# Small jobs inside the attention stage, each issued in two pieces behind two output quads instead of whole behind one, in a new order

## The chip, the core and the metric

The kernel runs on one core of a Trainium2 chip, in one launch. The metric is the device time in microseconds: the median of three runs of the kernel before is 269.8 us (269.74 to 269.80). Engines are named as in the profile: PE is TensorE's matrix multiplication, PEld its weight loads, ACT ScalarE, DVE VectorE, POOL GpSimd, SP SyncE, which issues the transfers.

## The reference

For 2 x 1024 tokens of width 128 the reference computes a gated feed-forward layer, causal attention, and the feed-forward layer again, each on a layer norm of x and each added to x:

```
x = x + 0.5 * ffn(layernorm(x));  x = x + attention(layernorm(x));  x = x + 0.5 * ffn(layernorm(x))

ffn:       gate from rms-normed logits of 8 experts (softmax, top 1, normalised to nearly 1)
           out = sum over e of (gelu(x @ w1[e] + b1[e]) @ w2[e] + b2[e]) * gate,   128 -> 256 -> 128
attention: q, k, v = split((xn * ln_w + ln_b) @ w_qkv), 8 heads of 8 columns; q and k to unit length
           softmax(8 * q @ k.T, causal) @ v, then @ w_out
```

All arrays are float32.

## The kernel before

**Groups and stages.** The 2048 tokens are four groups of 512 (four tiles of 128). The first layer runs group by group over 16 chunks of hidden units (three matmuls up, three down, with every operand in a high and a low part). Its last chunks run into the attention stage, and the second layer follows with the same 16-chunk loop. The second layer's groups are numbered 4 to 7 (`GROUPS` is 4).

**The attention stage** is a list of 80 steps, two to a *quad step*, so 40 quad steps. A unit is one group's queries with four of the heads. There are eight units: 3, 3, 7, 7, 3, 3, 7, 7 quad steps long, and two units make a pair (pairs start at quads 0, 6, 20 and 26, called `q1`, `q2`, `q3` from the second on). A step is: scores on PE (L708) into one of three sets of PSUM banks, the exponential on ACT (L937), for blocks on the causal diagonal a mask on POOL (L1527, L1533), and for both steps of a quad together the product with the values on PE (L746, for a unit's last quad, the corners, L740). The scores of a step wait until the exponential three steps earlier is done. A unit's last quad has small exponentials (128x256 instead of 128x1024). PE's program is fixed: in quad step k it issues the scores of steps 2k and 2k + 1 and then the output of quad k - 3, called here the output behind those scores. At the end of a unit the output stands between the two scores instead.

**The jobs** (`jobs`, `fill`, `empty`) are small pieces of other work that PE does behind the output of a given quad, into one spare PSUM bank: the transposes of the fourth group's normalised tokens (`"ln"`), its q, k, v products in two halves (`"qkv"`), the output projections of an earlier pair in two halves (`"project"`), and the transposes for the second layer's first group (`"ffn_ln"`). DVE empties the bank after each (`empty`), and runs `output(pair)` before the first job of a pair: it transposes the pair's outputs out of PSUM (`o_copied`), divides, and transposes back (`o_ready`), which is what the projections read. The bank is one, so `fill(n)` begins with `pe.wait_ge(job_emptied, n)`: all earlier jobs must have been emptied. DVE's order is the loop over `jobs` at the end of its program, with the work that each `if` adds behind a job: behind the second `qkv` half stand squares, sums, the guess and nine Newton operations, and the unit vectors (`own_squares` to `unit_vectors`), then `stacks`, which the transposing DMAs for pair 3's scores read. Behind other jobs stand statistics and normalising of the second layer's groups (`first_stats`, `normalise`, L1028, L1037, L1044) and `turn_features`, a DVE transpose that SP sends through DRAM to transposed features. POOL takes the reciprocal root of the variance (`ln_once`) in its own fixed place among the masks.

Of the kernel before, what the change touches and what calls it, by code (L numbers as in the profile page):

```python
# [30 lines left out]
P = 128  # L31
# [3 lines left out]
GROUP_TILES = 4  # L35
# [13 lines left out]
QUADS = 2  # L49
# [34 lines left out]
AT_FIRST = dict(AT, gate_product=6, gate_logits=6, gate_shift=11, gate_tanh=13, gate_weight=14, ln_copy=4, ln_low=8,  # L84
# [27 lines left out]
def build(nc, x, ln_w, ln_b, w_qkv, w_out, gate_w, gate_b, rms_w, w1, b1, w2, b2, out):  # L112
# [9 lines left out]
    with ctx:  # L122
# [128 lines left out]
        for st in steps:  # L251
# [13 lines left out]
        jobs = [(q1, "ln", LAST), (q1 + 2, "project", (0, 0)), (q1 + 4, "project", (0, 1)),  # L265
                (q1 + 5, "qkv", 0), (q1 + 7, "qkv", 1), (q2 + 3, "ffn_ln", 0),
                (q2 + 5, "project", (1, 0)), (q3, "project", (1, 1)),
                (q3 + 2, "project", (2, 0)), (q3 + 4, "project", (2, 1)),
                (quad_steps, "project", (pairs - 1, None))]
        assert len({at for at, *_ in jobs}) == len(jobs)  # L270
# [25 lines left out]
        def job_bank(n):  # L296

            at = jobs[n][0]
            return 13 - output_bank(steps[2 * min(at, quad_steps - 1)]["unit"] // QUADS)

        def pair_of_job(n):
            return steps[2 * min(jobs[n][0], quad_steps - 1)]["unit"] // QUADS
# [241 lines left out]
        def _(pe):  # L544
# [82 lines left out]
            def ffn_group(layer, g):  # L627
# [5 lines left out]
                for c in range(CHUNKS):  # L633
# [12 lines left out]
                    if layer == 1 and first and c == 3:  # L646
                        fill(len(jobs) - 1)
# [65 lines left out]
            def pv(k):  # L713
# [10 lines left out]
                if opens and pair > 1:  # L724
                    pe.wait_ge(job_emptied, sum(at < k for at, *_ in jobs))
# [26 lines left out]
            def fill(n):  # L752

                at, kind, arg = jobs[n]
                bank = ps[:, job_bank(n), :]
                if n:
                    pe.wait_ge(job_emptied, n)
                gates = sum(quad < at for quad in gate_at)
                if gates:
                    pe.wait_ge(gate_logits_done, GROUPS + gates)  # L760
                if n == 0 or pair_of_job(n) != pair_of_job(n - 1):
                    pe.wait_ge(o_copied, pair_of_job(n))
                tiles = [slice(P * i, P * i + P) for i in range(GROUP_TILES)]
                if kind in ("ln", "ffn_ln"):
                    norm = ATT if kind == "ln" else FFN
                    pe.wait_ge(xn_done[norm], GROUP_TILES * (LAST + 1 if kind == "ln" else GROUPS + 1))
                    for i, tile in enumerate(tiles):
                        m = pe.transpose(bank[:, tile], xn[:, norm, i, :], ident[:, :])
                elif kind == "qkv":
                    for i in halves[arg]:  # L770
                        m = pe.matmul(bank[:, 192 * (i % 2):192 * (i % 2) + 192], xf[:, ATT, tiles[i]], wqkv_sb[:, :],
                                      start=True, stop=True)
                elif kind == "project":
                    pair, half = arg
                    pe.wait_ge(o_ready, pair + 1)
                    for tile in tiles if half is None else [tiles[i] for i in halves[half]]:
                        m = pe.matmul(bank[:, tile], o_feat[:, tile], wout_sb[:, :], start=True, stop=True)  # L777
                m.then_inc(job_filled, 1)


# [24 lines left out]
            next_job = 0  # L805

# [12 lines left out]
            def outputs(k):  # L819

                nonlocal next_job
                for quad in range(max(pv_until(k - 1), 0), pv_until(k)):
# [5 lines left out]
                    if jobs[next_job][0] == quad:  # L828
                        fill(next_job)
                        next_job += 1  # L830
                    if quad in gate_at:
                        pe.wait_ge(job_emptied, next_job)
# [189 lines left out]
        def _(dve):  # L1022
# [162 lines left out]
            def ffn_group(layer, g):  # L1185
# [7 lines left out]
                for c in range(CHUNKS):  # L1193
# [194 lines left out]
            for n, (at, kind, arg) in enumerate(jobs[:-1]):  # L1388
# [6 lines left out]
                if (kind, arg) == ("project", (0, 1)):  # L1395
# [168 lines left out]
```

## Time and profile before

| | |
|---|---|
| median of 3 runs | 269.8 us |
| the profiled execution, its own time | 269.82 us |
| its span, first to last instruction | 268.1 us |
| first layer, to the first exponential | 104.7 us |
| attention stage, to ACT's table load for the second layer | 67.9 us (104.7 to 172.5) |
| second layer | 95.6 us |
| granted TensorE clock | 0.998 of full speed (2.4 GHz) |
| PE, DVE, ACT, POOL busy | 258.2, 216.2, 217.5, 80.7 us |

What is timed is the execution, 269.82 us. The span is what the instructions cover, and 1.7 us lie around it. In a timeline row the first number is the start, the second how long the merged instructions were busy, xN how many records there are, and brackets give the idle time before and what ended it. A float32 matmul is two records (two passes), so "x4" for a projection half is two matmuls. Records on PE overlap, so the distance between the starts of two rows says more of a cost than the busy time does.

### The profile page before, as it was taken

To read this page: it belongs to the slowest core of one execution; us is meant where nothing else is said; L and a number is where in the kernel's file an instruction comes from. 1 tells how busy PE (TensorE), PEld (TensorE's weight loads), DVE (VectorE), ACT (ScalarE), POOL (GpSimd) and SP (SyncE) were. 2 spreads that over 40 slices of the span, in tenths; PEclk is the share of its full clock that TensorE was granted. 3 is DMA by queue.
4 is the path that set the end of the run, shared out by engine and by line. 5 is a ranking of instruction groups with operands and counts; after the bars stand their busy time and mean duration, and the time that the engine had idled before them with its cause. 6 is when DMAs were issued, how large, how long until landed. Compare 5 with 4: busy or idle time off the path is not lost.

```text
span 268.1 us, 5428 instructions
## 1 busy us (share of the span) xinstructions
PE 258.2 (96%) x1829; PEld 183.6 (69%) x1829; DVE 216.2 (81%) x590; ACT 217.5 (81%) x344; POOL 80.7 (30%) x175
## 2 busy tenths in 40 slices
PE   7999999999999999979998999999999999999995
PEld 6886878888788786533434433378888887888783
DVE  7999899998898987797378587378889678697784
ACT  2897668859878889999999999987777867859673
POOL 6302104204850482664349545520200000200100
PEclk9999999999999999999999999999999999999999
DMA  5741200001012104101314003300004211210311
GB/s 152 219 123 23 58 1 2 0 1 39 2 34 46 42 2 78 40 1 22 62 39 82 2 4 78 80 1 4 0 8 111 42 39 39 39 34 9 80 39 39
DMA packets 33343, 11.51 MB, mean 43 GB/s; under 512 B 24130, under 2 KB 32548, under 8 KB 33316
## 3 DMA queue, kind: packets, MB, share of 16 engines
q1 hardware_dynamic: 33172, 11.11, 17.7%
q8 instruction: 14, 0.23, 0.4%
q14 instruction: 13, 0.11, 0.1%
q10 hardware_dynamic: 144, 0.07, 0.1%
HBM read 4.88 MB, written 2.62 MB: 28 GB/s over the span
## 4 chain that ended last, share of the span: by engine, by line
PE 73%; DVE 8%; ACT 7%; issue 5%; POOL 4%; DMA 2%; SPq 0%; POOLq 0%; DVEq 0%; ACTq 0%
PE ps L590 10%; PE ps L596 10%; PE ps L608 10%; PE ps L593 10%; PE ps L613 10%; PE ps L611 9%; PE ps L746 5%; ACT probs L937 3%; PE ps L708 2%; PE ps L777 2%; ACT h L924 2%; POOL probs L1533 1%; POOL w_raw L1527 1%; DMA kT<-k_stack 1%; DVE h_lo L1100 1%
## 5 line engine op out<-in xcount | busy, mean ns | idle before, releaser
L924 ACT ACTIVATE h<-ps,cols 128x512 f32<-128x512 f32 x128 | 88.0, 694 | 36.2 <-PE ps L596 32.6
L1100 DVE TENSOR_TENSOR h_lo<-h,h_hi 128x512 fp32r<-128x512 f32 x128 | 88.6, 698 | 19.1 <-ACT h_hi L927 16.7
L937 ACT ACTIVATE probs<-ps 128x1024 f32<-128x1024 f32 (+1 forms) x80 | 65.0, 918 | 1.5 <-PE ps L708 1.4
L590 PE MATMUL ps<-xT_hi,w_hi 128*128 128x512 f32 x128 | 51.5, 402 | 0.0
L608 PE MATMUL ps<-h_hi,w_hi 128*128 128x512 f32 x128 | 50.5, 395 | 0.3 <-ACT yT L949 0.3
L927 ACT ACTIVATE h_hi<-ps,cols 128x512 fp32r<-128x512 f32 x73 | 50.2, 688 | 0.0
L613 PE MATMUL ps<-h_lo,w_hi 128*128 128x512 f32 x128 | 50.2, 392 | 0.0
L596 PE MATMUL ps<-xT_lo,w_hi 128*128 128x512 f32 x128 | 49.9, 390 | 0.0
L593 PE MATMUL ps<-xT_hi,w_lo 128*128 128x512 f32 x128 | 49.9, 390 | 0.0
L611 PE MATMUL ps<-h_hi,w_lo 128*128 128x512 f32 x128 | 49.9, 389 | 0.0
L746 PE MATMUL ps<-probs,v_ones 128*32 128x512 f32 (+4 forms) x384 | 34.2, 458 | 0.9 <-POOL probs L1533 0.6
L1436 POOL TENSOR_TENSOR gate_rms<-gate_ms,neg_half 128x4 f32<-128x4 f32 x8 | 9.7, 1217 | 72.8 <-DVE gate_ms L1065 72.7
L608 PEld LDWEIGHTS ps<-h_hi,w_hi 128*128 128x128 f32 x128 | 24.0, 188 | 6.3 <-ACT yT L949 0.7
L613 PEld LDWEIGHTS ps<-h_lo,w_hi 128*128 128x128 f32 x128 | 24.0, 188 | 6.0 <-DVE h_lo L1100 0.9
L590 PEld LDWEIGHTS ps<-xT_hi,w_hi 128*128 128x128 f32 x128 | 24.0, 188 | 5.7 <-issue 0.7
L596 PEld LDWEIGHTS ps<-xT_lo,w_hi 128*128 128x128 f32 x128 | 24.0, 188 | 5.2
L611 PEld LDWEIGHTS ps<-h_hi,w_lo 128*128 128x128 f32 x128 | 24.0, 188 | 4.8
L593 PEld LDWEIGHTS ps<-xT_hi,w_lo 128*128 128x128 f32 x128 | 24.1, 188 | 4.5
L1098 DVE CAST h_hi<-h 128x512 fp32r<-128x512 f32 x55 | 23.4, 426 | 3.9 <-ACT h L924 3.1
L1533 POOL TENSOR_SCALAR_AFFINE_SELECT probs<-probs 128x128 f32<-128x128 f32 x64 | 18.0, 312 | 21.2 <-ACT probs L937 20.8
L708 PE MATMUL ps<-qT,kT 32*64 32x64 f16 (+5 forms) x320 | 19.9, 266 | 2.3 <-ACT probs L937 1.1
L708 PEld LDWEIGHTS ps<-qT,kT 32*128 32x128 f16 (+1 forms) x320 | 7.2, 96 | 20.1 <-ACT probs L937 12.4
(141 smaller groups left out, 273.2 us busy)
## 6 DMA issues: line engine op xcount, KB each, us to landing
w_raw<-in_L_ffn_w SPq DMA_DIRECT2D x8, 256.0 KB, 4.6
turned<-blocks SPq DMA_DIRECT2D x6, 256.0 KB, 2.0
w_raw<-turned SPq DMA_DIRECT2D x24, 64.0 KB, 2.3
w_raw<-v_ones SPq DMA_DIRECT2D x8, 128.0 KB, 2.4
x_sb<-in_L_attn_x SPq DMA_DIRECT2D x3, 256.0 KB, 6.8
out_x<-x_sb SPq DMA_DIRECT2D x3, 256.0 KB, 2.3
w_raw<-o_scaled SPq DMA_DIRECT2D x2, 256.0 KB, 4.3
x_sb<-in_L_attn_x SPq DMA_DIRECT2D x2, 128.0 KB, 2.3
```

What stands on the lines that cost most here:

```text
L590: pe.matmul(bank, w1_hi[:, w], xT_hi[:, cols_g], start=True, stop=False)
L593: pe.matmul(bank, w1_lo[:, w], xT_hi[:, cols_g], start=False, stop=False)
L596: pe.matmul(bank, w1_hi[:, w], xT_lo[:, cols_g], start=False, stop=True).then_inc(up_done, 1)
L608: pe.matmul(y, w2_hi[:, w], h_hi[:, c % RING, :], start=(c == 0), stop=False)
L611: pe.matmul(y, w2_lo[:, w], h_hi[:, c % RING, :], start=False, stop=False)
L613: pe.matmul(y, w2_hi[:, w], h_lo[:, c % RING, :], start=False, stop=(c == CHUNKS - 1)).then_inc(down_done, 1)
L708: m = pe.matmul(ps[first_row:first_row + keys, 2 * score_set(s) + hd, at:at + width], kT[rows, kp, st["quad"], k0:k0 + keys], qT[rows, p, ...
L746: m = pe.matmul(ps[ROW * j:ROW * j + ROW, bank, q0:q0 + width], v_ones[:, SEQ // P * st["b"] + kt, 4 * st["quad"] + j, :], probs[:, (s + j ...
L924: first = nc.scalar.activation(h[:, slot, :], ps[:, BANK_H + slot, :], ACT.Gelu, bias=bias)
L927: nc.scalar.activation(h_hi[:, slot, :], ps[:, BANK_H + slot, :], ACT.Gelu, bias=bias).then_inc(gelu_done, 1)
L937: nc.scalar.activation(probs[:, s % P_SLOTS, :, 0:width], ps[:, bank:bank + 2, 0:width], ACT.Exp, scale=SCALE).then_inc(exp_done, 1)
L1100: dve.tensor_tensor(h_lo[:, slot, :], h[:, slot, :], h_hi[:, slot, :].bitcast(f32), ALU.subtract).then_inc(split_done, 1)
```

## The change

Each job has two quads instead of one. `fill(n, piece)` issues the first half of the job behind the output of its first quad and the second half behind its second quad. The wait for the bank stands ahead of the first piece, and the count that releases DVE (`job_filled`) behind the second. The order of jobs changes:

| job | quad before | quads after |
|---|---|---|
| ln (fourth group) | 6 | 6, 7 |
| qkv first half | 11 | 8, 10 |
| qkv second half | 13 | 11, 12 |
| project (0,0) | 8 | 13, 14 |
| project (0,1) | 10 | 15, 17 |
| project (1,0) | 25 | 21, 23 |
| project (1,1) | 26 | 24, 25 |
| ffn_ln | 23 | 27, 28 |
| project (2,0) | 28 | 31, 32 |
| project (2,1) | 30 | 34, 35 |

The last job, project (3), stays behind chunk 3 of the second layer. The first gate product moves from quad 24 to 30, its tanh on ACT from step 62 to 72. DVE: `stacks` of the fourth group moves behind the emptying of project (0,0), the normalising of group 4 behind (1,1), and the normalising and turning of group 6 leave the attention stage for chunk 1 of the second layer. In that layer's first group ACT's copy of features moves from chunk 4 to 9, DVE's low part from 8 to 10. POOL: the roots for groups 4 and 5 stand together behind the masks of quad 25, that of group 6 behind all masks.

```diff
+AT_FIRST = dict(AT, gate_product=6, gate_logits=6, gate_shift=11, gate_tanh=13, gate_weight=14, ln_copy=9, ln_low=10,
                 ln_stats=(5, 6), ln_aggregate=7, ln_normalise=(12, 13))
...
+        jobs = [((q1, q1 + 1), "ln", LAST), ((q1 + 2, q1 + 4), "qkv", 0), ((q1 + 5, q1 + 6), "qkv", 1),
+                ((q1 + 7, q1 + 8), "project", (0, 0)), ((q1 + 9, q1 + 11), "project", (0, 1)),
...
+        pieces_at = {quad: (n, piece) for n, (quads, *_) in enumerate(jobs[:-1]) for piece, quad in enumerate(quads)}
-        gate_at = {q2 + 4: GROUPS, quad_steps - 3: GROUPS + 1}
+        gate_at = {q3 + 4: GROUPS, quad_steps - 3: GROUPS + 1}
-        TANH_AT = 62
+        TANH_AT = 72
...
-            def fill(n):
+            def fill(n, piece):
+                quads, kind, arg = jobs[n]
                 bank = ps[:, job_bank(n), :]
-                if n:
-                    pe.wait_ge(job_emptied, n)
...
+                if piece == 0:
+                    if n:
+                        pe.wait_ge(job_emptied, n)
+                    gates = sum(quad < quads[0] for quad in gate_at)
+                    if gates:
+                        pe.wait_ge(gate_logits_done, GROUPS + gates)
+                    if n == 0 or pair_of_job(n) != pair_of_job(n - 1):
+                        pe.wait_ge(o_copied, pair_of_job(n))
...
                 elif kind == "qkv":
-                    for i in halves[arg]:
-                        m = pe.matmul(bank[:, 192 * (i % 2):192 * (i % 2) + 192], xf[:, ATT, tiles[i]], wqkv_sb[:, :],
-                                      start=True, stop=True)
+                    i = halves[arg][piece]
+                    m = pe.matmul(bank[:, 192 * piece:192 * piece + 192], xf[:, ATT, P * i:P * i + P], wqkv_sb[:, :],
+                                  start=True, stop=True)
...
-                m.then_inc(job_filled, 1)
+                if piece:
+                    m.then_inc(job_filled, 1)
...
                     pv(quad)
-                    if jobs[next_job][0] == quad:
-                        fill(next_job)
-                        next_job += 1
+                    if quad in pieces_at:
+                        fill(*pieces_at[quad])
...
+                        if c == 1:
+                            normalise(FFN, GROUPS + 2, 2)
+                            turn_features(GROUPS + 2)
...
                 if (kind, arg) == ("qkv", 1):
                     own_squares(LAST)
...
                     unit_vectors(dve, LAST)
+                if (kind, arg) == ("project", (0, 0)):
                     stacks(LAST)
```

PE's program behind the outputs of quads 14 and 15, before (`ps<-qT,kT` is scores, `ps<-probs,v_ones` an output):

```order
L746 MATMUL ps<-probs,v_ones 32x512 x4
L708 MATMUL ps<-qT,kT 128x320 x2
L708 MATMUL ps<-qT,kT 128x192 x2
L708 MATMUL ps<-qT,kT 128x320 x2
L708 MATMUL ps<-qT,kT 128x192 x2
L746 MATMUL ps<-probs,v_ones 32x512 x4
L708 MATMUL ps<-qT,kT 64x64 x8
L746 MATMUL ps<-probs,v_ones 32x512 x4
```

and after, where L778 is a piece of a projection:

```order
L747 MATMUL ps<-probs,v_ones 32x512 x4
L778 MATMUL ps<-wout_sb,o_feat 128x128
L709 MATMUL ps<-qT,kT 128x320 x2
L709 MATMUL ps<-qT,kT 128x192 x2
L709 MATMUL ps<-qT,kT 128x320 x2
L709 MATMUL ps<-qT,kT 128x192 x2
L747 MATMUL ps<-probs,v_ones 32x512 x4
L778 MATMUL ps<-wout_sb,o_feat 128x128
L709 MATMUL ps<-qT,kT 64x64 x8
L747 MATMUL ps<-probs,v_ones 32x512 x4
```

The first L778 is the second piece of project (0,0), behind quad 14. The second is the first piece of project (0,1), behind quad 15 and ahead of a corner's scores; being a first piece, it carries a wait for the bank. Nothing stood in either place before.

DVE's program at the end of the fourth group's chain, before:

```order
L413 SCALAR_TENSOR_TENSOR rnorm<-newton,rnorm 128x64
L440 TENSOR_TENSOR qkn<-qk_raw,rnorm 128x512
L1182 CAST q_stack<-qkn 128x32x16
L1182 CAST k_stack<-qkn 128x64x8
L456 TENSOR_TENSOR q_stack<-qkn,q_stack 128x32x8
L456 TENSOR_TENSOR k_stack<-qkn,k_stack 128x32x8
L1044 TENSOR_SCALAR xn<-x_sb,mean_var,rstd 128x128 x4
```

and after (L1353 is the emptying of a projection):

```order
L413 SCALAR_TENSOR_TENSOR rnorm<-newton,rnorm 128x64
L440 TENSOR_TENSOR qkn<-qk_raw,rnorm 128x512
L1353 TENSOR_TENSOR x_sb<-ps,x_sb 128x256
L1178 CAST q_stack<-qkn 128x32x16
L1178 CAST k_stack<-qkn 128x64x8
L456 TENSOR_TENSOR q_stack<-qkn,q_stack 128x32x8
L456 TENSOR_TENSOR k_stack<-qkn,k_stack 128x32x8
L1353 TENSOR_TENSOR x_sb<-ps,x_sb 128x256
```

The emptying of project (0,0) has come between the chain and the stacks; before, both halves of that projection were emptied ahead of the fourth group's copies.

## Rows read from the trace of the kernel before

**Rows 1.** Windows of four stretches, busy us and instructions of each engine

```profile
104.70:172.60 67.90, 63.56 (x887) 26.70 (x886) 45.99 (x152) 66.33 (x86) 36.02 (x101) 1.00 0.18 38
...
180.00:200.00 20.00, 20.00 (x94) 16.67 (x93) 16.74 (x42) 14.92 (x25) 1.73 (x2) 1.00 0.00 1
```

**Rows 2.** Waits between 120 and 173 us: total, times, longest

```profile
PEld ps L708 <- ACT probs L937: 11.3, 17, 0.8
```

**Rows 3.** Timeline of ACT in narrow windows: start, us, instruction, [idle before]

```profile
119.59 4.73 ACT L937 ACTIVATE probs<-ps 128x1024 f32<-128x1024 f32 x5
...
126.90 4.22 ACT L937 ACTIVATE probs<-ps 128x256 f32<-128x256 f32 x5 [0.47 <-PE ps L708]
...
137.76 1.59 ACT L937 ACTIVATE probs<-ps 128x1024 f32<-128x1024 f32 x3
...
139.38 1.03 ACT L937 ACTIVATE probs<-ps 128x1024 f32<-128x1024 f32 x1
...
162.68 9.82 ACT L937 ACTIVATE probs<-ps 128x1024 f32<-128x1024 f32 x12
```

**Rows 4.** Timeline of PE, first half of the attention stage

```profile
121.27 0.66 PE L768 MATMUL ps<-ident,xn 128*128 128x128 f32 x4
...
124.78 0.71 PE L777 MATMUL ps<-wout_sb,o_feat 128*128 128x128 f32 x4
125.42 0.25 PE L708 MATMUL ps<-qT,kT 32*64 32x64 f16 x8
...
126.60 0.58 PE L708 MATMUL ps<-qT,kT 32*64 32x64 f16 x12
...
128.75 0.40 PE L708 MATMUL ps<-qT,kT 32*128 32x512 f16 x4
129.08 1.07 PE L746 MATMUL ps<-probs,v_ones 128*32 128x320 f32 x16
130.08 0.92 PE L771 MATMUL ps<-wqkv_sb,xf 128*128 128x192 f32 x4
130.93 0.40 PE L708 MATMUL ps<-qT,kT 32*128 32x512 f16 x4
131.25 0.64 PE L740 MATMUL ps<-w_raw 128*32 128x128 f32 x16
```

**Rows 5.** Timeline of PE, the last projection job

```profile
182.07 1.05 PE L777 MATMUL ps<-wout_sb,o_feat 128*128 128x128 f32 x8
182.87 0.47 PE L590 MATMUL ps<-xT_hi,w_hi 128*128 128x512 f32 x1
```

**Rows 6.** Timeline of PE where the after-job scores of 138.6 us stand

```profile
138.61 0.92 PE L708 MATMUL ps<-qT,kT 32*64 32x64 f16 x16
```

**Rows 7.** Timeline of DVE: a projection's add, then the fourth group's chain

```profile
125.52 0.42 DVE L1354 TENSOR_TENSOR x_sb<-ps,x_sb 128x256 f32<-128x256 f32 x1
...
134.70 0.42 DVE L1339 COPY qk_raw<-ps 128x256 f32<-128x256 f32 x1 [2.98 <-PE ps L771]
...
141.08 0.52 DVE L1182 CAST q_stack<-qkn 128x512 f16<-128x512 f32 x1
```

**Rows 8.** Timeline of DVE: statistics, normalising, the output's first transpose

```profile
142.96 1.10 DVE L1044 TENSOR_SCALAR xn<-x_sb,mean_var,rstd 128x128 f32<-128x128 f32 x4
143.99 0.70 DVE L1310 STREAM_TRANSPOSE o_blocks<-ps 128x512 f32<-128x512 f32 x1
...
156.67 0.87 DVE L1028 BATCH_NORM_STATS2 bn_part<-x_sb 128x6 f32<-128x128 f32 x4
157.58 0.38 DVE L1037 BATCH_NORM_AGGREGATE mean_var<-bn_part 128x2 f32<-128x6 f32 x4
```

**Rows 9.** Timeline of PE, later jobs

```profile
153.80 1.06 PE L746 MATMUL ps<-probs,v_ones 128*32 128x512 f32 x8 [0.19 <-DVE x_sb L1354]
```

**Rows 10.** Timeline of DVE in the first group of the second layer

```profile
179.32 0.71 DVE L1310 STREAM_TRANSPOSE o_blocks<-ps 128x512 f32<-128x512 f32 x1
```

**Rows 11.** Timeline of PE there

```profile
185.48 0.39 PE L613 MATMUL ps<-h_lo,w_hi 128*128 128x512 f32 x1
```

More of the change, by code:

```diff
@@ L264, in build @@
         q1, q2, q3 = first_of_pair[1:]
[L265 to L270, printed above, removed]
+        jobs = [((q1, q1 + 1), "ln", LAST), ((q1 + 2, q1 + 4), "qkv", 0), ((q1 + 5, q1 + 6), "qkv", 1),
+                ((q1 + 7, q1 + 8), "project", (0, 0)), ((q1 + 9, q1 + 11), "project", (0, 1)),
+                ((q2 + 1, q2 + 3), "project", (1, 0)), ((q2 + 4, q2 + 5), "project", (1, 1)),
+                ((q3 + 1, q3 + 2), "ffn_ln", 0), ((q3 + 5, q3 + 6), "project", (2, 0)),
+                ((q3 + 8, q3 + 9), "project", (2, 1)), ((quad_steps, quad_steps), "project", (pairs - 1, None))]
         job_number = {(kind, arg): n for n, (_, kind, arg) in enumerate(jobs)}
-        gate_at = {q2 + 4: GROUPS, quad_steps - 3: GROUPS + 1}
+        pieces_at = {quad: (n, piece) for n, (quads, *_) in enumerate(jobs[:-1]) for piece, quad in enumerate(quads)}
+        gate_at = {q3 + 4: GROUPS, quad_steps - 3: GROUPS + 1}
         LATER_GATES = {0: GROUPS + 1, 2: GROUPS + 2, 3: GROUPS + 3}
-        TANH_AT = 62
+        TANH_AT = 72
         def gate_of(layer, g):
@@ L296, in job_bank @@
         def job_bank(n):
-            at = jobs[n][0]
+            at = jobs[n][0][0]
             return 13 - output_bank(steps[2 * min(at, quad_steps - 1)]["unit"] // QUADS)
         def pair_of_job(n):
-            return steps[2 * min(jobs[n][0], quad_steps - 1)]["unit"] // QUADS
+            return steps[2 * min(jobs[n][0][0], quad_steps - 1)]["unit"] // QUADS
         by_dma = [("features", F) for F in range(GROUPS + 1, 2 * GROUPS)] + [("y", F) for F in range(GROUPS, 2 * GROUPS - 1)]
@@ L724, in pv @@
                 if opens and pair > 1:
-                    pe.wait_ge(job_emptied, sum(at < k for at, *_ in jobs))
+                    pe.wait_ge(job_emptied, sum(quads[1] < k for quads, *_ in jobs))
                     pe.wait_ge(gate_logits_done, GROUPS + sum(quad < k for quad in gate_at))
@@ L775, in fill @@
                     pe.wait_ge(o_ready, pair + 1)
-                    for tile in tiles if half is None else [tiles[i] for i in halves[half]]:
-                        m = pe.matmul(bank[:, tile], o_feat[:, tile], wout_sb[:, :], start=True, stop=True)
-                m.then_inc(job_filled, 1)
+                    for i in halves[piece] if half is None else halves[half][piece:piece + 1]:
+                        m = pe.matmul(bank[:, P * i:P * i + P], o_feat[:, P * i:P * i + P], wout_sb[:, :], start=True, stop=True)
+                if piece:
+                    m.then_inc(job_filled, 1)
             def keep_busy(times):
@@ L827, in outputs @@
                     pv(quad)
-                    if jobs[next_job][0] == quad:
-                        fill(next_job)
-                        next_job += 1
+                    if quad in pieces_at:
+                        fill(*pieces_at[quad])
                     if quad in gate_at:
-                        pe.wait_ge(job_emptied, next_job)
+                        pe.wait_ge(job_emptied, sum(quads[1] <= quad for quads, *_ in jobs))
                         gate_product(gate_at[quad], 13 - output_bank(steps[2 * quad]["unit"] // QUADS))
@@ L1387, in _ @@
             normalise(ATT, LAST, LAST)
-            for n, (at, kind, arg) in enumerate(jobs[:-1]):
+            for n, (_, kind, arg) in enumerate(jobs[:-1]):
                 if n == 0 or pair_of_job(n) != pair_of_job(n - 1):
```

46 lines of the change are left out of this document (17 added, 29 removed).

## The prediction

> **What bounds the kernel now.** First the table of windows by stage. In the second layer PE has no idle time and ACT and DVE do, so PE sets the pace. In the attention stage, where nearly all of the edit lies, ACT is busy 66.3 of 67.9 us and PE 63.6 [rows 1]. The waits say which is the slower: PE's weight loads for the scores wait for exponentials 17 times, 11.3 us in total [rows 2]. So ACT paces the stage and PE runs ahead of it, by the three sets of banks at most. Then ACT's timeline in narrow windows, for the pace itself: five big exponentials in 4.73 us with the last of them about 1.1 long is 0.90 each. In the row of three at 137.76, two small ones follow a big one at 0.90 and the next exponential starts at 139.38, 1.62 later, so a small one takes about 0.26 and about 0.19 is lost at this unit's end [rows 3]. What the change can give back is only what ACT loses beyond that pace. From 139.38 to 162.68 lie 28 exponentials (steps 40 to 67), 22 big and 6 small: 22 x 0.904 + 6 x 0.264 + 0.13 for a tanh = 21.6 us, where 23.3 passed, so 1.7 us are lost [rows 3]. The clearest loss is earlier: the small exponential at 126.90 had waited 0.47 [rows 3], for scores that stand behind an output, which stands behind a projection of 0.64 us [rows 4].
>
> **What a piece costs.** Whole jobs, by the distance of starts: projection 124.78 to 125.42, 0.64; qkv half 130.08 to 130.93, 0.85; the four transposes 0.59 (busy 0.66, less the 0.07 by which the projection's busy time also passes its distance) [rows 4]. How much of that is not work shows in the last projection job: eight records took 0.80 where four took 0.64, but it is followed by matmuls of its own shape (128 wide), not by scores of 32 rows [rows 5]. So a record is worth about 0.10 and 0.24 of the four-record job is fixed. The Trainium skill has the reason, in "TensorEngine Tiling (Array Packing)", under Key Properties of Tiling Modes: changing the tiling mode drains TensorE. The rows fit that. If only records cost, a piece would be half a job, 0.32, the chain below would be 0.4 us shorter, and the sum 0.4 lower.
>
> I take 0.43 for half a projection, 0.52 for one product of a qkv half, 0.37 for two transposes. No row shows one alone; the ends are half a job (0.32, no fixed part) and 0.13 more than I take (0.56, near the whole). Ten jobs in pieces add 6 x 0.22 + 2 x 0.19 + 2 x 0.15 = 2.0 us to PE. Most of it is covered while PE waits for ACT (11.3 us of such waits), and single pieces fit: a full quad costs PE 0.33 for scores and 1.00 for the output (128.75, 129.08, 130.08) [rows 4], with a piece 1.76, under ACT's 1.81. That is the good side: a whole projection makes 1.97.
>
> **The first part, to the fourth group's products.** From the first transposes at 121.27 on PE: 0.37, then 1.33 + 0.37, 1.33 + 0.52, so the corner's scores at 125.19 (before 125.42), 0.23 early. From the second set of corner scores at 126.60 to the next scores at 128.75 it was 2.15 with a projection of 0.64; with a product of 0.52 it ends at 128.40. Then 1.33 + 0.52 = 130.25 (before 130.93), 0.33 for scores, 0.58 for the corner output (131.25 on), 0.52: the second products are done at T = 131.68. Before it was 134.6, so the chain behind it starts 2.9 us earlier [rows 4, 7].
>
> **The step that decides.** Behind project (0,0) comes project (0,1), at quad 15, and its first piece waits until project (0,0) is emptied. DVE empties that only after the fourth group's chain. In the trace the chain from the first copy to the end of the unit vectors lasts 134.70 to 141.08, 6.38 us, and a projection's add 0.42 [rows 7]. So the bank is free at 131.68 + 0.10 + 6.38 + 0.42 + 0.02 = 138.60. PE comes to the wait after two quads with a piece and one without: 131.68 + 1.76 + 1.76 + 1.33 = 136.53. It stands 2.07 us. Queued behind it are the scores of the unit's corner and everything after. Those come at 138.60 + 0.43; 0.18 for them (125.42's row less overlap), 1.00 for the output, and the second corner scores and those of the next unit start at 140.21. Before, they started at 138.61 [rows 6], so 1.6 late. At a corner reached late like this, ACT's next big exponential starts 0.61 behind (126.60 to 126.90, and a small one of 0.31): 140.82 instead of 139.38 [rows 3, 4, 6]. This is +1.44 us. Bounds: if T comes 0.5 us sooner (pieces at half price) +0.9; if each of the six pieces before T costs 0.13 more, +2.2. More waiting by ACT elsewhere before this point is free, since the chain on DVE hides it.
>
> **Behind it.** Of the 1.7 us lost between 139.38 and 162.68 about 0.6 is the end of three units, which stays. The rest hangs on whole jobs late in the stage: transposes, the gate product, two projections behind one another with the wait of 0.19 for an emptying [rows 9], two more. Pieces fit under ACT's pace, so I give back 0.7 and not the full 1.1, because a new wait comes in. The transposes at quad 27 need `o_copied`, and DVE reaches that transpose only after the emptying of (1,1), a normalising of 1.1 and statistics of 0.87 + 0.3, then its own 0.70 [rows 8]. With (1,1) done at 152.64 on the old clock, that is 152.7 + 0.44 + 1.15 + 1.20 + 0.72 = 156.2, and PE arrives at 152.64 + 0.5 (the wait of quad 26's output) + 1.00 + 1.33 = 155.5. It stands 0.7; ACT, with big exponentials queued, sees little of it, but a unit's end follows. Then the tanh falls outside this stretch, +0.13, and the piece at quad 32 now stands between a corner's output and a full one, which I price at +0.2. Together -0.7 + 0.3 = -0.4.
>
> The moved stacks end at about 138.6 + 2.0 = 140.6 (they take 141.08 to 142.96), where they ended by 142.96 before, and the scores that need them come later than before, not earlier, so their transfers are no wait: 0 [rows 7, 8]. Second layer: normalising (1.1) and turning (0.7, as L1310) come upon DVE behind output(3), which starts at 179.32 and occupies it about 2.2 us [rows 8, 10]. Then chunk 5's low part is due at 185.48, when PE starts the matmul that reads it [rows 11]: DVE reaches it at 179.32 + 2.2 + 0.6 + 1.8 = 183.9 and ends at 184.6. That hides it, with 0.9 us left. If the cover is gone it costs up to 1.
>
> **Sum.** The profiled execution took 269.82 us, its span 268.1. Change: +1.44 - 0.4 = +1.04. Predicted 270.9 us; the median of the runs shown, 269.8, is the same to 0.02.
>
> **Rivals.** *Faster: the wait never bites.* If the bank is free before PE arrives, the pieces do what their size suggests. From the first part ACT is 0.5 early at 139.38 and 0.4 comes later: 268.9. It decides at DVE's chain: it would have to last 2.1 us less than the 6.8 shown. Against it, the chain is fifteen operations that depend on one another, behind three copies, and PE is late by at most 0.5. Chance 0.12. *No change.* The wait costs nearer to 0.9, with the full 1.1 given back afterwards: 269.8 + 0.9 - 1.1 + 0.3 = 269.9. For it, bounds on both sides are real. Chance 0.17. *Slower still.* The wait at quad 27 is seen in full (+0.7), and DVE's backlog in the second layer reaches PE (+0.5): 272.1. For it, DVE order is fixed and both stand behind long groups of work. Chance 0.14. That leaves 0.57 for the forecast.
>
> **The numbers.** Less than 0.2%, 0.54 us, can't be told from no change here. The forecast's own range is 270.1 to 271.7; from bounds, 0.9 - 1.1 + 0.3 is +0.1 and 2.2 - 0.4 + 0.7 is +2.5. The range for 8 in 10 is 269.5 to 272.2, leaving out the faster case and the end of the slow one. Slower by over 0.2%: the forecast's 0.57, of which 0.03 falls short, and the slow rival 0.14, and so 0.68; the same 0.20, faster 0.12.
>
> **What would show it.** In the new profile, PE's wait before a piece of L778 with DVE's L1353 as its end, some 2 us, near 136.5 to 138.6; the next big exponential near 140.8; a single projection piece to the next scores 0.43; the second products done near 131.7; PE waiting for o_blocks before the transposes of ffn_ln, 0.7; PE without idle time in the second layer, and its length unchanged at 95.6 us within 0.2. It is wrong if that first wait is under 1 us, or if ACT reaches step 40 before 140, or if the second layer grows.

## The result, and the profile after

The changed kernel took 271.61 us (median of 6 runs, 271.51 to 271.70), the kernel before 269.78 on the same chip (6 runs, 269.74 to 269.87). The ratio is 1.0067, with an interval of 1.0054 to 1.008. It is slower by 1.83 us, where +1.1 was forecast against that median; the time lies inside the stated range, 269.5 to 272.2. Times here are medians of fast executions; of the kernel with the gate's transpose moved (below) one execution of 629.66 us, in the slow state, is left out. The profiled execution took 271.70 us with a span of 269.9; 1.8 us of span came in, so the span holds the whole difference.

The line numbers move a little: PE's scores, outputs, projections, qkv products and transposes are L709, L747, L778, L772 and L769 now, ACT's exponential is L933, DVE's add of a projection L1353, POOL's diagonal mask L1531. The windows of the same two stretches (span of the stretch, then busy us and instructions of PE, its weight loads, DVE, ACT and POOL, granted clock, DMA share, GB/s):

```profile
104.70:173.64 68.94, 64.29 (x887) 26.76 (x886) 42.79 (x147) 66.02 (x85) 35.98 (x98) 1.00 0.16 33
180.00:200.00 20.00, 20.00 (x94) 16.68 (x93) 18.36 (x46) 14.24 (x24) 1.61 (x2) 1.00 0.12 27
```

Beside [rows 1]: ACT's load of its next table, which ends the attention stage, starts at 173.64 where it started at 172.52, ACT is busy for about as long as before, and PE still has no idle time in the second layer (20.00 of 20.00 us). From the first matmul of the second layer to the end it was 94.45 us and is 94.44. So all that is lost is lost before that matmul (it stood at 173.61, and stands at 175.50: +1.89).

The waits between 120 and 175 us (total, times, longest) answer [rows 2]:

```profile
PEld ps L709 <- ACT probs L933: 6.7, 13, 0.8
...
ACT probs L933 <- PE ps L709: 2.6, 5, 0.8
...
PEld ps L747 <- POOL probs L1531: 2.0, 5, 1.1
...
PE ps L778 <- DVE x_sb L1353: 1.4, 1, 1.4
```

PE's waits for exponentials fell from 11.3 us to 6.7, as they would if pieces fill what was slack. The last line is the wait that the prediction put at quad 15. PE's timeline there (start, us, instruction, and in brackets the idle time before it with its end):

```profile
131.32 0.59 PE L772 MATMUL ps<-wqkv_sb,xf 128*128 128x192 f32 x2
131.84 0.47 PE L709 MATMUL ps<-qT,kT 32*128 32x512 f16 x4
...
133.66 0.49 PE L709 MATMUL ps<-qT,kT 32*128 32x448 f16 x8
...
135.50 0.48 PE L709 MATMUL ps<-qT,kT 32*128 32x320 f16 x8
135.91 1.07 PE L747 MATMUL ps<-probs,v_ones 128*32 128x512 f32 x8
138.40 0.49 PE L778 MATMUL ps<-wout_sb,o_feat 128*128 128x128 f32 x2 [1.42 <-DVE x_sb L1353]
138.81 0.26 PE L709 MATMUL ps<-qT,kT 32*64 32x64 f16 x8
...
139.99 0.59 PE L709 MATMUL ps<-qT,kT 32*64 32x64 f16 x16
```

and DVE's, whose chain of the fourth group ends ahead of the add that frees the bank:

```profile
131.95 0.42 DVE L1338 COPY qk_raw<-ps 128x256 f32<-128x256 f32 x1 [2.59 <-PE ps L772]
...
137.31 0.69 DVE L440 TENSOR_TENSOR qkn<-qk_raw,rnorm 128x512 f32<-128x512 f32 x1
137.92 0.42 DVE L1353 TENSOR_TENSOR x_sb<-ps,x_sb 128x256 f32<-128x256 f32 x1
```

The add ends at 138.34 and the piece starts at 138.40. ACT's timeline, in narrow windows, shows what becomes of it: the small exponentials at 139.12 and 140.30 wait 0.8 each, and the big one of step 40, which stood at 139.38 [rows 3], starts at 140.61, +1.23. Step 68, at 162.68 before, starts at 163.11.

```profile
139.12 0.38 ACT L933 ACTIVATE probs<-ps 128x256 f32<-128x256 f32 x1 [0.83 <-PE ps L709]
...
140.61 1.02 ACT L933 ACTIVATE probs<-ps 128x1024 f32<-128x1024 f32 x1
...
163.11 1.03 ACT L933 ACTIVATE probs<-ps 128x1024 f32<-128x1024 f32 x1
...
165.04 1.02 ACT L933 ACTIVATE probs<-ps 128x1024 f32<-128x1024 f32 x1
...
167.36 1.02 ACT L933 ACTIVATE probs<-ps 128x1024 f32<-128x1024 f32 x1 [0.37 <-PE ps L709]
```

Of these, 163.11 to 165.04 is 1.93 us for two big exponentials and 165.04 to 167.36 is 2.32, where the same two gaps had been 1.82 and 1.81. PE's timeline shows the first reason, at quad 31:

```profile
162.73 1.07 PE L747 MATMUL ps<-probs,v_ones 128*32 128x320 f32 x16
164.22 0.46 PE L778 MATMUL ps<-wout_sb,o_feat 128*128 128x128 f32 x2 [0.42 <-issue]
164.61 0.40 PE L709 MATMUL ps<-qT,kT 32*128 32x512 f16 x4
```

"Issue" names no releaser, but the piece waits by the program for the gate product's bank to be read, and DVE reads it at just that time, behind a normalising and a turning:

```profile
161.66 1.51 DVE L1040 TENSOR_SCALAR xn<-x_sb,mean_var,rstd 128x128 f32<-128x128 f32 x4
163.21 0.71 DVE L1103 STREAM_TRANSPOSE blocks<-xn 128x512 f32<-128x512 f32 x1
163.85 0.27 DVE L1052 STREAM_TRANSPOSE gate_rows<-ps 128x128 f32<-128x128 f32 x1
```

The normalising itself is slow here: four tiles take 1.51 us from 161.66, beside four masks of POOL between 161.26 and 163.57, where the four from 154.31 take 1.11. Those 0.40 us are nearly the whole of the piece's wait of 0.42. No run moves them, so that they cause it is not shown.

The last loss stands at the very end of the stage, on POOL. The exponentials are done before 173.64, and the last big output waits for two diagonal masks. First the kernel before, PE's and POOL's timelines:

```profile
172.61 1.07 PE L746 MATMUL ps<-probs,v_ones 128*32 128x320 f32 x16
```

```profile
172.01 0.54 POOL L1533 TENSOR_SCALAR_AFFINE_SELECT probs<-probs 128x128 f32<-128x128 f32 x2 [0.38 <-ACT probs L937]
```

and the changed one, PE, POOL (each mask in a window of its own) and DVE:

```profile
174.50 1.07 PE L747 MATMUL ps<-probs,v_ones 128*32 128x320 f32 x16 [0.82 <-POOL probs L1531]
```

```profile
173.14 0.58 POOL L1531 TENSOR_SCALAR_AFFINE_SELECT probs<-probs 128x128 f32<-128x128 f32 x1 [0.38 <-ACT probs L933]
...
173.67 0.77 POOL L1531 TENSOR_SCALAR_AFFINE_SELECT probs<-probs 128x128 f32<-128x128 f32 x1
```

```profile
173.17 0.39 DVE L1117 CAST xT_hi<-w_raw 128x512 fp32r<-128x512 f32 x1
173.60 0.69 DVE L423 TENSOR_TENSOR xT_lo<-w_raw,xT_hi 128x512 fp32r<-128x512 f32 x1
```

Two masks took 0.54 together and take 1.31. What changed is DVE's company: the high and low features of group 5 (L1117, L423) had run at 167.86 and 168.32, in slack, and now run beside the masks. They don't wait for what they read, which was turned at 163.21. They come late by their place in DVE's order, behind the emptying of project (2,1), which moved from quad 30 to 34 and 35 and ends at 170.94, and behind `gate_weight` and the statistics.

The whole loss in one ledger, start to start: +1.23 up to step 40; -0.80 from step 40 to 68 (22.50 us where 23.30 passed, 0.13 of it the tanh that left this stretch); +0.11 and +0.51 over steps 68 to 72; +0.07 from there to the load of ACT's table (the same tanh now stands in it); +0.77 from the table load to the last big output. The sum is +1.89, which is what the first matmul of the second layer shows.

### The profile page after: what moved, and what is told of

It reads as the page before. It is cut to its first block, busy times and chain, and to the rows that moved or that the text cites. A ratio compares the mean times of both kernels' runs of the same rounds, so it can differ in the third digit from the quotient of the medians.

```text
span 269.9 us, 5427 instructions
## 1 busy us (share of the span) xinstructions
PE 259.6 (96%) x1829; PEld 184.5 (68%) x1829; DVE 214.9 (80%) x590; ACT 217.1 (80%) x344; POOL 83.0 (31%) x175
## 4 chain that ended last, share of the span: by engine, by line
PE 76%; ACT 7%; DVE 6%; issue 5%; POOL 3%; DMA 1%; POOLq 0%; DVEq 0%; ACTq 0%
PE ps L590 10%; PE ps L596 10%; PE ps L608 10%; PE ps L593 10%; PE ps L613 9%; PE ps L611 9%; PE ps L747 7%; ACT probs L933 4%; PE ps L709 3%; POOL probs L1531 2%; ACT h L920 1%; POOL w_raw L1525 1%; PE ps L778 1%; PE ps L741 1%; DVE h_lo L1096 1%
## 5 line engine op out<-in xcount | busy, mean ns | idle before, releaser
L933 ACT ACTIVATE probs<-ps 128x1024 f32<-128x1024 f32 (+1 forms) x80 | 64.9, 922 | 2.9 <-PE ps L709 2.8
L747 PE MATMUL ps<-probs,v_ones 128*32 128x512 f32 (+4 forms) x384 | 34.2, 458 | 1.5 <-POOL probs L1531 1.5
L1531 POOL TENSOR_SCALAR_AFFINE_SELECT probs<-probs 128x128 f32<-128x128 f32 x64 | 19.7, 337 | 25.8 <-ACT probs L933 25.5
L709 PE MATMUL ps<-qT,kT 32*64 32x64 f16 (+5 forms) x320 | 18.9, 267 | 1.4 <-ACT probs L933 0.6
L747 PEld LDWEIGHTS ps<-probs,v_ones 128*32 128x32 f32 x384 | 9.2, 109 | 13.9 <-issue 6.9
```

The costliest lines, as they stand in the source:

```text
L709: m = pe.matmul(ps[first_row:first_row + keys, 2 * score_set(s) + hd, at:at + width], kT[rows, kp, st["quad"], k0:k0 + keys], qT[rows, p, ...
L747: m = pe.matmul(ps[ROW * j:ROW * j + ROW, bank, q0:q0 + width], v_ones[:, SEQ // P * st["b"] + kt, 4 * st["quad"] + j, :], probs[:, (s + j ...
L933: nc.scalar.activation(probs[:, s % P_SLOTS, :, 0:width], ps[:, bank:bank + 2, 0:width], ACT.Exp, scale=SCALE).then_inc(exp_done, 1)
```

## The experiments

Each time is a median of 4 to 11 executions. The kernel before had a median of 269.77 to 269.82 us beside them, so times are compared with 271.61 and 269.8 throughout. Each interval reaches some 0.3 us to either side, so that a smaller difference between two experiments tells little without the trace.

**The bank freed early.** The theory: quad 15's piece waits for DVE's chain, and that costs most of the loss. The add that empties (0,0) is put behind the first of three Newton rounds; nothing else moves.

```diff
 guesses(LAST)
-inverse_lengths(dve, LAST)
-unit_vectors(dve, LAST)
+inverse_lengths(dve, LAST, range(1))
 ...
 if (kind, arg) == ("project", (0, 0)):
+    inverse_lengths(dve, LAST, range(1, 3))
+    unit_vectors(dve, LAST)
     stacks(LAST)
```

> The changed kernel, with DVE emptying project (0,0) after the first of the three Newton rounds of the fourth group instead of after its unit vectors. In the changed kernel PE stood from 136.9 to 138.4 us before the first piece of project (0,1), and step 40's exponential came 1.23 us later than before. Theory W (the wait for the bank is the largest cost): PE has no wait there, step 40 starts near 138.9 (1.7 earlier than in the changed kernel), the later part gives back less since there is less to give, and the time falls by 1.0 to 1.7 us, to 270.0 to 270.6. Rival P (the price is the 2 us of added work of the pieces on PE, and the wait only stands where PE would lose it anyway): the wait goes and the time falls by under 0.3 us, to 271.3 or more.

Measured: 270.08 us (ratio to before 1.0011, 1.0002 to 1.002), 1.53 less than the changed kernel. PE's timeline, the same piece:

```profile
136.76 0.49 PE L778 MATMUL ps<-wout_sb,o_feat 128*128 128x128 f32 x2
137.18 0.25 PE L709 MATMUL ps<-qT,kT 32*64 32x64 f16 x8
```

and ACT's:

```profile
138.98 1.02 ACT L933 ACTIVATE probs<-ps 128x1024 f32<-128x1024 f32 x1
```

No wait is left, and step 40 starts 0.40 before the old 139.38. So the wait cost 1.53, more than the 1.23 that step 40 is late, because it also hid a small gain of the first part. It doesn't make the kernel faster than before by itself, as the rival of a wait that never bites had it: other costs remain.

**The features early again.** The theory: the masks stretch because DVE works beside them. `early_features` moves ahead of `gate_weight`.

```diff
 if (kind, arg) == ("project", (2, 1)):
+    early_features(GROUPS + 1)
     gate_weight(GROUPS)
 ...
-early_features(GROUPS + 1)
 gate_logits(GROUPS + 1)
```

> The changed kernel, with DVE's cast and subtraction for the features of group 5 put right behind the last projection of the attention stage, ahead of the gate weight and the statistics of group 6. In the changed kernel these two ran at 173.2 to 174.3 us, beside POOL's last diagonal masks, which took 0.58 and 0.77 us instead of 0.29, and PE's second last output came at 174.50, 0.77 later than ACT's end alone would give. Theory M (DVE's operations from SBUF to SBUF in their fast form hold up POOL's masks, and these are on the path): the last two masks take 0.29 each, the second last output comes near 173.7, and the time falls by 0.6 to 0.8 us, to 270.8 to 271.0. Rival L (POOL's masks are late for another reason, or the up matmuls wait for ACT's last exponentials and table load, whatever the masks do): masks get shorter or not, and the time stays within 0.2 us of 271.6.

Measured: 270.77 us (1.0039, 1.0027 to 1.0052), 0.84 less. POOL's timeline and DVE's:

```profile
171.10 1.48 POOL L1531 TENSOR_SCALAR_AFFINE_SELECT probs<-probs 128x128 f32<-128x128 f32 x4 [0.37 <-ACT probs L933]
172.93 0.54 POOL L1531 TENSOR_SCALAR_AFFINE_SELECT probs<-probs 128x128 f32<-128x128 f32 x2 [0.35 <-ACT probs L933]
```

```profile
170.66 0.42 DVE L1117 CAST xT_hi<-w_raw 128x512 fp32r<-128x512 f32 x1
171.11 0.83 DVE L423 TENSOR_TENSOR xT_lo<-w_raw,xT_hi 128x512 fp32r<-128x512 f32 x1
```

The last two masks take 0.54 again. The stretch hasn't gone: it follows the two operations to the masks at 171.10, where PE has other work.

**The same cost put into the kernel before.** If the company of these two operations is the cause, the old kernel must pay for it too. There they are held back until the masks of step 76 are done.

```diff
+dve.wait_ge(mask_done, masks_until[76])
 early_features(GROUPS + 1)
```

> The kernel before, with one edit: DVE's cast and subtraction for the features of group 5 wait until the mask of step 76 is done, so that they stand beside the last two diagonal masks, as in the changed kernel. Nothing else moves. Theory M: the last two masks (0.29 each before, 172.0 to 172.6 us) stretch to 1.0 to 1.4 us together, PE's second last output comes 0.5 to 0.8 us later and the time rises by 0.5 to 0.8, to 270.3 to 270.6. Rival L: the time stays at 269.8, since the masks had time to spare or the two engines don't hold each other up.

Measured: 270.31 us (1.0017, 1.0008 to 1.0026), +0.49. POOL, DVE, and PE:

```profile
172.22 0.99 POOL L1534 TENSOR_SCALAR_AFFINE_SELECT probs<-probs 128x128 f32<-128x128 f32 x2 [0.38 <-ACT probs L937]
```

```profile
171.87 0.43 DVE L1121 CAST xT_hi<-w_raw 128x512 fp32r<-128x512 f32 x1 [4.07 <-POOL probs L1534]
172.33 0.72 DVE L423 TENSOR_TENSOR xT_lo<-w_raw,xT_hi 128x512 fp32r<-128x512 f32 x1
```

```profile
173.26 1.07 PE L746 MATMUL ps<-probs,v_ones 128*32 128x320 f32 x16 [0.50 <-POOL probs L1534]
```

One of the two masks is stretched (0.99 for both, 0.54 before), PE waits 0.50, and the kernel is 0.49 slower. With the experiment before it, this shows the cause from both sides.

**The gate's transpose ahead of the turning.** The theory: the piece at quad 31 waits for DVE's read of the gate product.

```diff
 normalise(FFN, GROUPS + 1, 1)
+gate_logits(GROUPS, job_bank(n), "transpose")
 turn_features(GROUPS + 1)
-gate_logits(GROUPS, job_bank(n))
+gate_logits(GROUPS, job_bank(n), "rest")
```

> The changed kernel, with DVE's transpose of the first gate product (the operation that PE's first piece of project (2,0) waits for) moved ahead of the turning of group 5's features. In the changed kernel that piece started at 164.22, 0.49 after its output had ended, and steps 68 to 74 took 6.19 us on ACT instead of 5.44 before, of which 0.13 is the tanh. Theory G (the late gate transpose pushes PE so far back that the quads 31 to 34 come late): the piece starts near 163.7, the steps 68 to 74 take 5.6 to 5.8 us, and the time falls by 0.4 to 0.6 us. Rival Q (the second piece, behind the corner's output at quad 32, and two outputs in a row make the loss by themselves): steps 70 to 72 still take 2.2 us or more and the time falls by under 0.2 us.

Measured: 271.20 us (1.0053, 1.0039 to 1.0066; the median of four executions), 0.41 less. PE's timeline has the piece right behind its output, which started at 162.59 and takes 1.00:

```profile
163.59 0.49 PE L778 MATMUL ps<-wout_sb,o_feat 128*128 128x128 f32 x2
```

The gap from step 68 to 70 is 1.81 again, that from 70 to 72 is 2.01 instead of 2.32. So 0.43 of the 0.62 lost there was this wait, and nearly all of it reaches the end. The other 0.20 goes with the piece at quad 32, between the outputs of a corner and of a full quad.

**Whole jobs in the new order.** The rival: the order, not the splitting, makes it slower. Each job stands whole behind its second quad.

```diff
-pieces_at = {quad: (n, piece) for n, (quads, *_) in enumerate(jobs[:-1]) for piece, quad in enumerate(quads)}
+pieces_at = {quads[1]: n for n, (quads, *_) in enumerate(jobs[:-1])}
 ...
-fill(*pieces_at[quad])
+fill(pieces_at[quad], 0)
+fill(pieces_at[quad], 1)
```

> The changed kernel in its new order of jobs, but each job whole, behind the output of its second quad. PE's work falls by some 2 us (ten pieces less, 0.2 each), and the first wait for the bank of project (0,1) moves from quad 15 to 17, behind DVE's chain, so it is gone. Theory W, with pieces of little worth: the time falls by 1.0 to 1.6 us, to 270.0 to 270.6, and the loss of ACT at step 25 is as large as before the change or smaller, because no job stands behind quad 9. Rival S (pieces give a gain of their own: whole jobs exceed ACT's 1.81 us for a quad and each costs 0.1 to 0.35): the wait goes but whole jobs lose 0.5 to 1 us in sum, so the time falls by 0.5 us or less.

Measured: 270.49 us (1.0029, 1.0018 to 1.004). Step 40 starts at 139.19: a job that begins one or two quads later finds its bank free. So in the changed kernel the splitting cost 1.12 us, but through waits that an earlier first piece runs into: the bank's, and the gate's too, for here steps 68 to 70 take 1.80. The masks stay stretched (the last two take 1.31 together), which fits the +0.7 against before.

**All three waits out.** The three edits above together.

> The changed kernel with three edits of DVE's order at once: the bank of project (0,0) emptied after the first Newton round, the features of group 5 split right behind the last projection, and the gate transpose ahead of the turning. If the three are separate costs on one path, the gains add: 1.53 and 0.84 as measured alone, and 0 to 0.5 for the third, so 268.7 to 269.3 us, under the kernel before (269.8). If pieces are a loss of their own (2 us more work on PE) that the waits only hid, the time stays above 269.8.

Measured: 268.86 us (0.9965, 0.9951 to 0.9978): faster than before by 0.9 us. The separate gains sum to 1.53 + 0.84 + 0.41 = 2.78, and 271.61 - 2.78 = 268.83, so they add up.

**The same with whole jobs.** What is splitting worth where nothing stands in its way? The three edits, with the edit of whole jobs.

> The three edits of DVE's order (bank, features, gate transpose) with whole jobs behind the second quad of each, in the new order: it differs from the run with the three edits only in that no job is split. Theory S (a piece fits beside an output within ACT's 1.81 us and a whole job does not): whole jobs cost 0.5 to 1.2 us in sum, so 269.4 to 270.0. Rival N (pieces are worth nothing, the order is): 268.7 to 269.0.

Measured: 269.82 us (1.000, 0.9991 to 1.0009), as before. Against 268.86 the pieces gain 0.96 us. The waits between 120 and 172 us, first with whole jobs, then the same two with pieces:

```profile
PEld ps L709 <- ACT probs L934: 12.3, 22, 0.8
...
ACT probs L934 <- PE ps L709: 1.5, 5, 0.4
```

```profile
PEld ps L709 <- ACT probs L933: 6.7, 13, 0.8
...
ACT probs L933 <- PE ps L709: 0.8, 3, 0.4
```

With pieces PE's waits for exponentials are 5.6 us less, of which some 1.8 is the pieces' own time (worked out in the last section) and the rest isn't explained here. ACT gets 0.7 of its idle time back.

**The pieces under the old order.** The rival: without the fourth group's projections first, pieces alone would do. Order of the kernel before: `ln`, (0,0), (0,1), then the two qkv halves, all in pieces.

```diff
-((q1 + 2, q1 + 4), "qkv", 0), ((q1 + 5, q1 + 6), "qkv", 1),
-((q1 + 7, q1 + 8), "project", (0, 0)), ((q1 + 9, q1 + 11), "project", (0, 1)),
+((q1 + 2, q1 + 3), "project", (0, 0)), ((q1 + 4, q1 + 5), "project", (0, 1)),
+((q1 + 6, q1 + 7), "qkv", 0), ((q1 + 8, q1 + 9), "qkv", 1),
```

DVE's `stacks` go back to their old place, right behind the unit vectors.

> The changed kernel with the first jobs in the old order, in pieces: ln (6, 7), project (0,0) (8, 9), project (0,1) (10, 11), qkv (12, 13) and (14, 15). No job waits for the bank behind DVE's chain, but the fourth group's products end some 5.7 us later than in the changed kernel, near 137.4. Theory O (the new order is there because pieces push the fourth group's products back, and pair 3's scores need its stacks by DMA): chain and stacks end near 146, their transfers near 150.5, where step 52's scores want them at 147.6, so PE waits about 2.5 us there and the time is 271.5 to 273. Rival: the transfers come in time, and without the wait at quad 15 the time is 270.0 to 270.6.

Measured: 275.87 us (1.023, 1.0216 to 1.0244), far above what was expected, and not by the expected way. PE did not wait for the stacks' transfers; it stood 2.77 us for `o_feat`, which DVE writes behind the late chain of the fourth group and its stacks:

```profile
148.99 0.72 PE L778 MATMUL ps<-wout_sb,o_feat 128*128 128x128 f32 x2 [2.77 <-DVE o_feat L1323]
...
151.70 1.94 PE L747 MATMUL ps<-probs,v_ones 128*32 128x448 f32 x16
```

Then the granted clock fell. Windows, with the clock as third value from the end:

```profile
140.00:149.00 9.00, 5.73 (x117) 2.68 (x109) 8.13 (x22) 7.49 (x10) 7.85 (x24) 1.00 0.25 48
149.00:154.00 5.00, 5.00 (x64) 2.56 (x64) 0.00 (x0) 2.71 (x4) 2.81 (x6) 0.50 0.37 67
154.00:160.00 6.00, 5.99 (x62) 2.22 (x61) 2.26 (x9) 4.77 (x6) 0.05 (x1) 0.84 0.00 0
```

At half clock for 5.0 us and at 0.84 for 6.0, PE does 2.5 + 1.0 = 3.5 us less than at full clock (an estimate from these rows). Steps 40 to 68 take 27.83 us here and 22.50 in the changed kernel, 5.33 more; so about 1.8 is left for the wait of 2.77, by this estimate, and the rest of it would be slack. Up to step 40 nothing is lost against before (139.39 for 139.38), and from step 68 to the last big output it is 11.39 us, as in the changed kernel, where it was 9.93 before: what the changed kernel loses behind step 68 (the gate's wait, quad 32, the tanh, the stretched masks), 1.46 of the +6.1, is still there. The cause of the wait is the order: with two quads for each job, the second qkv half is finished behind quad q1+9 instead of q1+7, and DVE reaches the first transpose of the output at 146.55, where it was 143.99 [rows 8]. So pieces alone, in the old order, are no way to the gain.

**Two attempts at the piece of quad 32.** On top of the three edits, the pieces of (2,0) go to quads 31 and 34, those of (2,1) to 35 and 36:

```diff
-((q3 + 5, q3 + 6), "project", (2, 0)),
-((q3 + 8, q3 + 9), "project", (2, 1)),
+((q3 + 5, q3 + 8), "project", (2, 0)),
+((q3 + 9, q3 + 10), "project", (2, 1)),
```

> The same three edits, and the pieces of project (2,0) behind quads 31 and 34 instead of 31 and 32, those of (2,1) behind 35 and 36. Theory Q (a piece between the corner's output of quad 32 and the full output of quad 33 makes scores for step 72 late, 0.5 us): steps 70 to 72 take 1.8 to 1.9 us instead of 2.3, and the time is 0.3 to 0.5 us under that of the run with the three edits alone. Theory G (the gate transpose made all of it): no difference within 0.15 us. If the later last projection makes DVE late for the second layer, it is slower.

Measured: 270.64 us (1.0032, 1.002 to 1.0045), slower by 1.78 than with the three edits alone. The gap from 70 to 72 is 1.81, as wanted, for 2.02. But DVE's gate work stands behind the emptying of (2,0), which is now later, and ACT, in order, stands before the tanh:

```profile
167.51 0.23 ACT L910 ACTIVATE gate_tanh<-gate_tmp 128x32 f32<-128x32 f32 x1 [1.29 <-DVE gate_tmp L1075]
```

and the features come beside the last masks again, 1.03 for two instead of 0.54. By the starts, steps 72 to 74 lose 1.46 (3.41 us for 1.95), the masks 0.49, and 0.2 is gained at quad 32, which is the 1.78 to 0.1:

```profile
172.38 1.03 POOL L1536 TENSOR_SCALAR_AFFINE_SELECT probs<-probs 128x128 f32<-128x128 f32 x2 [0.38 <-ACT probs L933]
```

So the tanh goes to step 74 and the features behind the first half of the gate work:

```diff
-TANH_AT = 72
+TANH_AT = 74
 ...
 gate_shift(GROUPS)
+early_features(GROUPS + 1)
 ...
-early_features(GROUPS + 1)
 gate_weight(GROUPS)
```

> The kernel with the last pieces spread over quads 31, 34, 35 and 36 and the bank and gate edits, with the tanh behind step 74 instead of 72 and the cast and subtraction of group 5's features right behind the gate shift. In the run before this one steps 70 to 72 had lost their 0.5 us (1.81 us for two), but ACT, in order, stood at the tanh of step 72 until DVE's gate shift had come behind the later emptying of project (2,0), 1.4 us, and a last mask took 0.78 beside the cast. Theory Q (the loss at quad 32 was real and was turned into the tanh's wait): no wait at the tanh, masks of 0.29, and 268.2 to 268.6 us, under the 268.86 of the three edits alone. Rival: the last projection, one quad later, holds up the gate product or DVE in the second layer, and the time is 268.9 or more.

Measured: 268.80 us (0.9962, 0.995 to 0.9975), which the runs can't tell from the 268.86 of the three edits. In the traces 0.13 of the 0.2 won at quad 32 is left: step 40 starts at 138.97 against 139.12, the last big output at 171.55 against 171.83. Where the rest went isn't settled; the four masks that start at 169.09 take 1.64 us beside the features at 168.94 and 169.40, against 1.48 for four with the three edits, which would be one place. The version to keep is the one with the three edits: 268.86 against 269.8 before, with fewer changes.

## Why the prediction was right, and which of its terms was not

It named slower, the place and the mechanism, and those held. That the total stayed inside the range is partly luck: its last term had the wrong sign, by 1.06 us, and 271.61 lies at the upper edge of the forecast's own range (271.7). By its own steps:

- **What a piece costs.** Forecast 0.43, 0.52 and 0.37. The single projection piece takes 138.40 to 138.81, 0.41; a qkv product 131.32 to 131.84, 0.52; a pair of transposes 0.37 (121.31 to 121.68). Right.
- **The fourth group's products done at T = 131.68.** The scores behind them start at 131.84: 0.16 late.
- **The deciding wait.** Forecast from 136.53 to 138.60, 2.07; measured 1.42, to 138.40. PE came 0.45 later: 0.16 from the start, the two quads with a piece took 1.82 and 1.84, not 1.76, and the one without took 1.48 (135.50 to 136.98), not 1.33. DVE was 0.2 earlier, since its chain from the first copy to the unit vectors took 6.05 (131.95 to 138.00), not 6.38. The 6.38 had three operations in it that ran long beside POOL's masks (L413 twice, 0.28 and 0.31 for 0.23; L440, 0.81 for 0.69). Step 40 came at 140.61, forecast 140.82; so +1.23 for +1.44. Right in kind; and freeing the bank gave 1.53 back. The criterion for being wrong, a first wait of under 1 us, was not met.
- **Given back to step 68.** 0.7 forecast, 0.80 measured, of which 0.13 is the tanh, so 0.67 of lost time. The size is right, the reason given for stopping short of 1.1 is not: the wait that the 0.7 had in it didn't show. The transposes at quad 27 start at 157.32, right behind their output of 156.29. DVE's transpose ended at 157.21, 1.0 later than forecast, but PE was 1.8 later, and so it missed the wait by 0.1 us.
- **Tanh and quad 32.** Forecast +0.13 + 0.2, measured +0.69 from step 68 to the table load. The 0.13 is a slip of the sum: the tanh moves from one stretch to the other, and the sum adds it where it arrives without taking it off where it left. The piece at quad 32 was priced right: 0.20 is left once the other wait is gone. The wait for the gate's transpose at quad 31, 0.43 in these gaps, was not in the sum.
- **Stacks' transfers and the second layer.** 0 and 0, and so it was: 94.45 and 94.44.
- **The term that failed** is the last, "-0.4" for all behind step 40. It came to +0.66 (-0.80 + 0.69 + 0.77). The largest part of that is 0.77 at the end of the stage, and the prediction had nothing there. It had followed DVE's moved operations only as far as who waits for their results, and found slack (0.9 us left for chunk 5, which was right: its low part ends at 186.43, and PE reads it at 187.36). It never asked what runs on POOL at the time to which they move. The trace of before could have told: masks of 0.54 for two with DVE idle or on statistics, and six masks at 123.53 that take 2.33 us beside the casts and products of `stacks`, where six at 159.82 take 1.56.

The faster rival's condition, the wait away, was met by an edit, and gave 270.08, not its 268.9. The runs show that number too, at 268.86, but only with all three waits out.

What the change did, then, as shown by whole runs: the new order with nothing in its way is worth 0 (269.82), the pieces -0.96, the bank's wait +1.53, the stretched masks +0.84, the gate's transpose +0.41. With the 0.04 of the first, that is +1.86 for the 1.83 measured.

## What to carry to other kernels

Cutting filler work into pieces pays where it is covered (here 0.96 us, for some 1.8 us more of PE's time), but it moves the first piece earlier, and whatever the job waits for must move with it: list for each job what its first instruction waits for, and put that release ahead of long chains on its engine. When an operation of DVE is moved, look not only at who reads its result but at what POOL does at the new time, above all at the end of a stage, where a stretched mask is on the path at once. Costs of this kind added up to 0.1 us here, so take each out alone, and judge the idea only with all of them gone.

## What the runs showed of the hardware

POOL's mask of 128x128 takes 0.29 us alone. Each one that a cast or a two-input operation of DVE from SBUF to SBUF lengthened took until that operation's end and about 0.15 more; in the twelve traces this holds for all 121 masks over 0.33 us, while masks beside the statistics or beside an add that reads PSUM take 0.29 to 0.30. In the changed kernel the first ends at 173.72, the cast at 173.56; the second at 174.44, the subtraction (two inputs in SBUF) at 174.29. In the old kernel with the features held back, the masks end at 173.21 and the subtraction at 173.05. The Trainium skill, in "SBUF — State Buffer", section "SBUF: two separate sides", has a rule for it: VectorE and GpSimd share a pair of ports. An operation of VectorE in a two-port mode takes it for its whole length, one with two inputs in SBUF does so against a GpSimd operation that reads SBUF, and whichever engine starts first blocks the other altogether. The traces agree with the blocking, with the three ends above, but not everywhere with who starts first: the mask of 173.14 starts 0.03 ahead of the cast of 173.17, by the trace, and is still the one that is held up.

A projection that stands between outputs and scores, which have other tile shapes, carries a fixed part. A piece of two matmuls takes 0.41 from start to start, a whole one of four 0.64; so two matmuls are 0.23, and 0.18 of each is fixed. The forecast had 0.24 from [rows 4, 5]. Ten jobs in pieces then add 6 x 0.18 for projections, 2 x 0.19 and 2 x 0.15 for the others, about 1.8 us (an estimate from these distances). PE's busy time hardly shows it: in 104.7 to 172 us it is 64.41 with the three edits and pieces, 63.76 with the three edits and whole jobs.

In the attention stage the granted clock fell to the lower of its two levels in one of the twelve traces, that of the pieces in the old order: PE had been busy 5.73 of 9.00 us and had stood for the last 2.77 of them; then it was 0.50 for 5 us, that is 1.2 GHz, and 0.84 over the next 6, a mix of both levels. A full output that takes 1.07 us took 1.94. PE's wait of 1.42 in the changed kernel did not do it (1.00 over the whole stretch). So a wait on the pacing engine cost more than its length here: 5.33 us from step 40 to 68, with a wait of 2.77. One execution of the kernel with the features early again (271.24 us) has a mean granted clock of 0.95 and no trace.
